# Attention in pairs of heads: GpSimd takes one head at a time, a third buffer for masked scores, and four bursts of half-width matmuls a pair

## What is computed

```
x = x + layernorm(attention(layernorm(x)))
x = x + layernorm(ffn(layernorm(x)))
```

```
q = rmsnorm(h @ Wq_a) @ Wq_b           # 128 features + 64 that are rotated by position (rope)
ckv = h @ Wkv_a;  kv = rmsnorm(ckv[:64]) @ Wkv_b;  k_pe = rope(ckv[64:])   # one k_pe for all heads
scores = (q . k) * 192**-0.5, causal;  p = softmax(scores);  o = p @ v;  out = concat(o) @ Wo
```

## Time and profile before

| | |
|---|---|
| median of 3 runs | 632.92 us (631.91 to 633.07) |
| the profiled execution | 632.73 us, of which its span is 630.8 us |
| mean granted clock of TensorE | 0.984 |
| PE busy | 590.5 us (94%) |
| DVE busy | 461.4 us (73%) |
| ACT busy | 400.0 us (63%) |
| POOL busy | 198.9 us (32%) |

### The profile page before, as it was taken

The page is one execution under the profiler, slowest core; times in us unless marked ns, Lnnn a source line. Parts: engine busy times, 40 slices in busy tenths (PEclk is TensorE's granted clock), DMA queues, the critical chain, the costliest instruction groups (busy, mean ns, idle before and its releaser), DMA issues.

```text
span 630.8 us, 10967 instructions
## 1 busy us (share of the span) xinstructions
PE 590.5 (94%) x3336; PEld 427.7 (68%) x3336; DVE 461.4 (73%) x1235; ACT 400.0 (63%) x1157; POOL 198.9 (32%) x172
## 2 busy tenths in 40 slices
PE   4786999999999999999999999999989999978996
PEld 4675767677677676776776767767658888754564
DVE  5876677677776777777767777777867888878466
ACT  4454677777777677766776777668753545264343
POOL 3134333443344334433353444344000000024630
PEclk9898999999999999999999999999989999999998
DMA  8100212312132122221331213205465000001003
GB/s 316 31 1 16 87 47 89 95 54 71 56 104 78 48 84 76 78 72 52 97 89 48 82 55 101 71 19 153 154 209 226 2 0 2 0 30 50 1 14 121
DMA packets 19561, 46.93 MB, mean 74 GB/s; under 512 B 2608, under 2 KB 3120, under 8 KB 19248
## 3 DMA queue, kind: packets, MB, share of 16 engines
q1 hardware_dynamic: 19504, 46.23, 22.8%
HBM read 39.80 MB, written 6.42 MB: 73 GB/s over the span
## 4 chain that ended last, share of the span: by engine, by line
PE 50%; issue 15%; DVE 15%; POOL 9%; ACT 9%; DMA 1%; POOLq 0%; SPq 0%; DVEq 0%; ACTq 0%
PE bank L1017 11%; PE bank L1019 9%; PE bank L1018 9%; PE bank L1072 7%; PE bank L1060 6%; POOL qrot L325 6%; ACT pr L407 3%; POOL qt_lo L332 3%; PE bank L1087 3%; DVE qswp L664 2%; DVE qrot L669 1%; DVE ss L677 1%; ACT pt L415 1%; DVE dot L865 1%; ACT qt_hi L397 1%
## 5 line engine op out<-in xcount | busy, mean ns | idle before, releaser
L677 DVE CUSTOM_DVE_ANT_0 ss<-bank,cst 128x128 f32<-128x128 f32 (+3 forms) x256 | 124.2, 490 | 95.6 <-PE bank L1019 75.0
L415 ACT ACTIVATE pt<-bank 128x128 f32<-128x128 f32 (+3 forms) x256 | 110.3, 431 | 88.4 <-PE bank L1060 88.3
L325 POOL TENSOR_TENSOR qrot<-qrot,qswp 64x512 f32<-64x512 f32 x64 | 81.9, 1280 | 208.2 <-DVE qrot L669 208.1
L407 ACT ACTIVATE pr<-ss,small 128x128 f32<-128x128 f32 (+3 forms) x256 | 142.4, 556 | 4.2 <-DVE small L677 4.0
L1060 PE MATMUL bank<-ident,pr 128*128 128x128 f32 x640 | 117.1, 281 | 0.6 <-ACT pr L407 0.6
L1017 PE MATMUL bank<-kt_hi,qt_hi 128*128 128x128 f32 (+3 forms) x256 | 101.0, 395 | 7.9 <-DVE small L677 4.5
L1060 PEld LDWEIGHTS bank<-ident,pr 128*128 128x128 f32 x640 | 74.5, 141 | 49.5 <-ACT pr L407 28.8
L332 POOL TENSOR_TENSOR qt_lo<-qrot,qt_hi 128x512 fp32r<-128x512 f32 x64 | 82.0, 1290 | 29.2 <-ACT qt_hi L397 27.9
L1072 PE MATMUL bank<-pt,kvn 128*64 128x256 f32 (+3 forms) x512 | 86.2, 448 | 0.7 <-ACT pt L415 0.7
L1019 PE MATMUL bank<-kt_hi,qt_lo 128*128 128x128 f32 (+3 forms) x256 | 82.9, 324 | 0.0
L1018 PE MATMUL bank<-kt_lo,qt_hi 128*128 128x128 f32 (+3 forms) x256 | 82.7, 323 | 0.0
(11 more groups left out here) (163 smaller groups left out, 1072.5 us busy)
## 6 DMA issues: line engine op xcount, KB each, us to landing
sv<-sv SPq DMA_DIRECT2D x16, 576.0 KB, 5.0
rsb<-rinv_scratch SPq DMA_DIRECT2D x64, 128.0 KB, 2.9
sq<-sq SPq DMA_DIRECT2D x16, 448.0 KB, 3.3
wvo_scratch<-vs SPq DMA_DIRECT2D x16, 256.0 KB, 4.8
wv_raw<-wvo_scratch SPq DMA_DIRECT2D x8, 512.0 KB, 4.8
xa<-x SPq DMA_DIRECT2D x8, 256.0 KB, 5.0
x<-x SPq DMA_DIRECT2D x1, 2048.0 KB, 9.6
out<-yo SPq DMA_DIRECT2D x8, 256.0 KB, 2.0
```

The lines of the kernel that those rows point to most:

```text
L325: nc.gpsimd.tensor_tensor(qrot[RKV:P, h, :], qrot[RKV:P, h, :], qswp[RKV:P, h, :], ALU.add)\
L407: nc.scalar.activation(pr[:, k % 4, 0:n], ss[:, k % 2, 0:n], ACT.Exp, bias=negmax[:, k % 8:k % 8 + 1], scale=-1.0, accum_out=rsum[:, k:k + ...
L415: nc.scalar.activation(pt[:, b, h, 0:i + 1, i * P:(i + 1) * P], bank[2 + k % 2][:, 0:(i + 1) * P].rearrange("p (j q) -> p j q", q=P), ACT. ...
L677: nc.vector.tensor_tensor_reduce(out=ss[:, k % 2, 0:n], in0=bank[k % 2][:, 0:n], in1=mask[:, SEQ - n:SEQ], scale=-SCALE, scalar=3.4e38, op ...
```

## The change

It has four parts. (1) POOL works head by head: add, then subtract, for head 0, then for head 1. (2) ACT makes the high part of head 0 one step earlier (k = 1 and 9 for 2 and 10; not so in the first half of the first pair), and copies `vs` at step 10 for 9. (3) `ss` has three buffers, chosen by `RING`; DVE waits for the exponents only where the buffer was used two units ago (k = 1 and 15). The third buffer takes room that was left free. (4) On PE, the last three blocks of `output` for sequence 1 stand together in step 2 (were: one in step 2, two in step 3), and `absorb_output` stands in step 9 directly ahead of `output` (was: step 8).

```diff
+RING = (0, 1, 2, 0, 1, 2, 0, 1, 2, 0, 1, 2, 0, 1, 2, 1)
+BACK = [next(d for d in range(1, 17) if RING[k - d] == RING[k]) for k in range(16)]
...
-    ss = att.take("ss", [P, 2, SEQ])
+    ss = att.take("ss", [P, 3, SEQ])
...
-    att.at += 32 + 4 * QB * 2 * RKV
+    att.at += 32
...
                 for b in (1,) if last else (1, 0):
-                    gi = 4 * p + (2 if b else 4)
-                    pool.wait_ge(a.qt_split, gi)
                     for h in range(2):
-                        add_rotated(gi + h, h)
-                    for h in range(2):
-                        query_lo(gi + h, b, h, gi + 2)
+                        gi = 4 * p + (2 if b else 4) + h
+                        pool.wait_ge(a.qt_split, gi)
+                        add_rotated(gi, h)
+                        query_lo(gi, b, h, gi + 1)
...
-                nc.scalar.activation(pr[:, k % 4, 0:n], ss[:, k % 2, 0:n], ACT.Exp, bias=negmax[:, k % 8:k % 8 + 1],
+                nc.scalar.activation(pr[:, k % 4, 0:n], ss[:, RING[k], 0:n], ACT.Exp, bias=negmax[:, k % 8:k % 8 + 1],
...
-                    if k in (2, 4):
-                        h = (k - 2) // 2
+                    if k in ((2, 4) if first else (1, 4)):
+                        h = k // 4
                         query_hi(4 * p + 2 + h, 1, h, None if first else PU * (p - 1) + UNITS + QB * (h + 1))
-                    if k in (10, 12) and not last:
-                        h = (k - 10) // 2
+                    if k in (9, 12) and not last:
+                        h = k // 12
                         query_hi(4 * p + 4 + h, 0, h, PU * p + QB * (h + 1))
-                    if k == 9:
+                    if k == 10:
                         act.wait_ge(a.wvo_made, p + 1)
...
-                if not first:
+                if BACK[k] == 2 and not first:
                     dve.wait_ge(a.exp_made, U - 1)
-                nc.vector.tensor_tensor_reduce(out=ss[:, k % 2, 0:n], in0=bank[k % 2][:, 0:n], in1=mask[:, SEQ - n:SEQ],
+                nc.vector.tensor_tensor_reduce(out=ss[:, RING[k], 0:n], in0=bank[k % 2][:, 0:n], in1=mask[:, SEQ - n:SEQ],
...
                     if k == 2 and not first:
-                        output(2 * p - 1, 1, [1])
-                    if k == 3 and not first:
-                        output(2 * p - 1, 1, [2, 3])
-                    if k == 8:
+                        output(2 * p - 1, 1, [1, 2, 3])
+                    if k in (5, 7) and not last:
+                        query(4 * p + 4 + k // 7, 0, k // 7, p + 1)
+                    if k == 9:
                         if last:
                             pe.wait_ge(a.wvo_moved, p)
                         else:
                             pe.wait_ge(a.wq_split, p + 2)
                         absorb_output(p)
-                    if k in (5, 7) and not last:
-                        query(4 * p + 4 + k // 7, 0, k // 7, p + 1)
-                    if k == 9:
                         output(2 * p, 0, [0], first)
```

## The result

| | before | after |
|---|---|---|
| median of 5 runs, us | 632.71 (631.54 to 633.07) | 635.46 (634.38 to 635.77) |
| span of the profiled execution, us | 630.8 | 632.6 |
| mean granted clock | 0.984 | 0.989 |
| a pair from the middle of the attention, us | 25.33 | 25.73 |

The ratio of after to before is 1.0047, with a 95% interval of 1.0034 to 1.0060. The forecast was 636.4 us and 25.7 us a pair.

A forecast was written before the change was run, and what follows sets the result against it. PE's list was taken to set the pace. Pair 0 at -1.6, pairs 1 to 14 at +0.41 each (+5.7) and pair 15 at -0.4 gave +3.7 us on 632.73, so 636.4 us; range 622 to 641.

The forecast's parts named there:

- The collision in `weights_lo`: Pairs 1 to 14: POOL's `query_lo` holds up DVE's subtractions with both inputs in SBUF, 0.95 us a pair.
- place A: PE's wait in step 5: scores of unit 7 held by unit 5's masking; expected to start 0.95 us later.
- The burst of step 2: Step 3's two `output` blocks join step 2's: 0.24 to 0.3 us less, waited off in step 5, counted 0.
- Place B: PE's wait in step 6: scores of unit 8 wait for head 0's `query_lo`; 0.3 us goes in pairs 1 to 14.
- The burst of step 9: `absorb_output` joins `output` in step 9 on PE: 0.24 us less in all 16 pairs.
- The sum of a pair: Pairs 1 to 14: +0.95 - 0.30 - 0.24 = +0.41 us each, +5.7 in all.
- The buffers: Third buffer removes most of DVE's wait for ACT (19.5 us in 31 places); PE waits in neither, counted 0.
- The first pair: Pair 0: PE starts 1.4 us earlier by POOL's order, and `absorb_output` brings 0.24: -1.6 us.
- The last pair: Pair 15, without `weights_lo`: 0.24 us for `absorb_output`, perhaps step 2's burst too; -0.4 us taken.
- rival 1: POOL comes first each time: 1.16 us a pair for 0.95, 639.3 us in all; chance 15%.
- rival 3: PE's longer idle makes the granted clock fall in half of the pairs: +12 us, 648 us; chance 6%.
- Rival 2: DVE's two subtractions get through before POOL starts: -0.54 us a pair, 623.1 us in all; chance 18%.

The follow-up runs named there:

- e1: Changed kernel with DVE's `weights_lo` doing its two subtractions from SBUF ahead of the two from the PSUM bank; 621.94 us, ratio to before 0.985.
- e2: Changed kernel with ACT making the high part of head 0 in step 2 again in the first half; 624.18 us, ratio to before 0.9875.
- e4: Kernel before with the PE bursts alone joined, and the copy of `vs` in step 10 for 9; 631.03 us, ratio to before 0.998.
- e6: e1 with `rotate_own` of head 1 put behind the masking of unit 5, not ahead of it; 615.22 us, ratio to before 0.9728.
- e8: e3 with, in the second half, ACT's high part of head 0 at k = 9 and the `vs` copy at k = 10; 626.71 us, ratio 0.9907.
- e5: e1 with two buffers for masked scores in place of three; 621.67 us, ratio to before 0.9835.
- e7: Changed kernel with ACT's high part of head 0 ahead of `weights_hi` in step 1; 629.10 us, ratio to before 0.9951.
- e3: Kernel before with POOL's order alone changed: add and subtract, head by head; 633.40 us, ratio to before 1.0024.

## Why the prediction was right

Mechanism, place and size of what decides held. By its own steps, of which the seventh and the ninth were wrong:

1. *The collision in `weights_lo`, +0.95 a pair.* Shown, at 0.98 (e1) and 0.99 (e2). The starts were placed on the same 0.01 us, and DVE went first by 0.01 or 0.02 in all 14 pairs: the first of the two subtractions took 0.29, POOL went in between, and the second ended 0.15 behind POOL. That DVE and not POOL was first is luck: the rows gave no reason for it, since the first pair shows only that POOL gets in between. What hung on it was 0.95 or 1.16, not the direction. The Trainium skill (SBUF — State Buffer, section "Who interferes with whom") says that a DVE instruction with two SBUF inputs contends with a GpSimd instruction that reads SBUF, and that the order of issue decides who blocks. The timeline agrees (0.29 for the one that was first, 1.28 for the one behind POOL), and in e1 and e2, where the two don't meet, both take 0.29. The section also says that a DVE instruction with at most one SBUF input does not contend with GpSimd; e1 agrees, where the rests from a bank ran beside POOL at their usual 0.29.
2. *It goes straight into place A.* Shown: the scores of unit 7 come 2.42 behind those of unit 6, for 1.15. That is 1.27, the 0.98 and the 0.29 of the next point.
3. *The burst of step 2, counted 0.* Shown by e4 (place A grows by the 0.29 saved) and e6 (a pair is shorter by all that place A loses).
4. *Place B, -0.30.* Shown by e8 at 0.30 (0.31 by the table), with no new wait behind it.
5. *The burst of step 9, -0.24.* Shown at 0.25: 3.67 for 3.92 from unit 10 to unit 12, in every kernel that has it. In e1 it and place B at 0.33 are the whole of the 0.58 under before.
6. *The sum of a pair, +0.41.* Measured +0.40 to +0.41: +1.27 in place A, -0.29, -0.32 and -0.25 for the rest.
7. *The buffers.* Their effect on the time was rightly 0 (e5), but the sentence that most of DVE's wait goes was wrong. The same wait over the whole span, to be held against the 19.5 in 31 of the earlier trace rows:

```profile
DVE ss L678 <- ACT pr L408: 18.2, 30, 0.6
```

   I read "31 times" as an average over all units. It is two places a pair, and these are k = 15 and k = 1, exactly where `BACK` is still two. Had I laid the count of the waits beside the list of `RING`, I should have seen that it frees the units that never waited.
8. *The first pair, -1.4 and -0.24.* Its timeline, answering to the earlier trace rows:

```profile
55.37 0.40 PE L1020 MATMUL bank<-kt_hi,qt_lo 128*128 128x512 f32 x1
56.28 1.26 POOL L327 TENSOR_TENSOR qrot<-qrot,qswp 64x512 f32<-64x512 f32 x1
57.13 0.57 DVE L653 TENSOR_TENSOR w_lo<-sq,w_hi 128x128 fp32r<-128x128 f32 x1
57.71 0.29 DVE L654 TENSOR_TENSOR w<-sq,w 64x128 fp32r<-64x128 f32 x1
...
58.05 0.50 PE L1018 MATMUL bank<-ql_hi,w_hi 128*128 128x512 f32 x1 [2.29 <-DVE w L654]
```

   POOL's addition for head 1 goes from 56.28 to 57.54. Only L653 is held by it, 0.28 us, as foreseen, and PE's wait is 2.29 instead of 3.75: 1.46 less, for 1.4.
9. *The last pair, -0.4.* Wrong: it takes about 0.14 more. The burst of step 2 does count, since place A has no `weights_lo` there (-0.29). But in step 8 PE now reaches its next transpose before the exponents are there, 0.86 behind L1020, where the first transposes of the earlier trace rows stand 0.17 behind the same kind of matmul. Before, `absorb_output` stood in that gap and covered it. The stretch from unit 7 to the last scores is 0.43 longer than before (12.84 for 12.41) although the burst of step 9 brings -0.24, so the wait costs 0.67. In the middle pairs two `query` blocks of steps 5 and 7 stand ahead of this point, which the last pair lacks. The timeline of step 8 there:

```profile
446.30 0.34 PE L1020 MATMUL bank<-kt_hi,qt_lo 128*128 128x384 f32 x1
447.16 0.27 PE L1082 MATMUL bank<-ident,small 128*8 128x128 f32 x1 [0.53 <-ACT pr L408]
```

   I had asked what covers step 8 for the middle pairs only.

The total, from the scores of unit 7 in the first pair to the last unit of the last: -1.46 and -0.24, 14 times +0.406, and +0.14 are +4.1. The two profiled executions differ by +4.2 over that stretch, for a forecast of +3.7. Their spans differ by less, +1.8, and the medians by +2.75, since three stretches outside it go the other way in these two executions:

- 1.04 up to the first scores (45.05 and 44.01). The code of that stretch is the same in all these kernels. It goes with the granted clock, which was at half for 6.83 us from 26.55 before, and for 3.41 us from 28.20 after; e4, with 6.83 as well, reaches the first scores at 45.27, and e7, with none ahead of them, at 43.02. Why the clock differed is open, and it says nothing of the change.
- 0.33 between the first scores and unit 7 of the first pair (11.12 and 10.79). e4, with the old order on POOL, has 11.13, and e3, with the new one alone, 10.91. So some 0.2 of it is a gain of POOL's order that my sum left out.
- 1.10 behind the attention. The windows of the same stretch, in the kernel before and then after, columns as in the earlier trace rows:

```profile
466.87:470.28 3.41, 3.31 (x8) 2.65 (x9) 2.60 (x5) 2.10 (x3) 0.00 (x0) 0.50 0.81 187
```

```profile
466.87:470.28 3.41, 0.81 (x4) 0.38 (x3) 1.58 (x3) 0.00 (x0) 0.00 (x0) 1.00 0.62 192
```

Before, the granted clock stood at half (1.2 GHz) for these 3.41 us; after, it stayed at full (2.4 GHz). No edit here was made to test this, and it isn't explained. The +2.75 of the medians lies between the +1.8 and the +4.2, so the closeness of 636.4 to 635.46 is in part luck: by the attention alone the kernel after would stand at 636.9.

Of the rivals, rival 1 (POOL first, 25.9 a pair) and rival 3 (the clock: it is 1.00 through all middle pairs, though PE stands 1.53 us in each) did not come. Rival 2's numbers did, in e1 and e2: the case in which the two don't meet, forecast at -0.54 a pair, measures -0.58. In e1 they miss each other by 0.03 us.

## What to carry to other kernels

When work is moved onto GpSimd at an earlier time, lay its start and end against VectorE's instructions with two SBUF inputs, and follow the one that may be held to the next wait of TensorE; if they meet, change VectorE's order so that the ones with a PSUM input fall beside GpSimd, which here turned a loss of 0.5% into a gain of 1.5% with one line. Do this for every place where the two engines' lists run side by side, the first and the last round too: the same line cost 0.6 us in the first pair. A saving on the busiest engine ahead of one of its waits is worth nothing until that wait is shortened, and the edit that shortened it (masking ahead of rotation) brought 0.59 us a pair, as much as all four parts of the change without the collision (0.58). Before a buffer is added, see which units wait, and whether the new ring gives those units a longer distance.

## What the runs showed of the hardware

- GpSimd's instruction that started 0.02 us behind L653 took 1.42 us in the trace, and 1.28 in e1 and e7, where nothing was in its way. An excess of 0.14 on GpSimd's side is all that shows there of a collision that costs VectorE 0.98; reading GpSimd's rows alone, one would pass over it.
- A GpSimd instruction that is waiting gets in between two VectorE instructions that stand 0.31 us apart from start to start and belong to the same engine's queue (313.57, 313.88): GpSimd doesn't wait until VectorE runs out of such work.
- TensorE stood idle 2.60 us at about 470 us in the changed kernel, and the granted clock did not fall:

```profile
470.04 0.50 PE L1018 MATMUL bank<-wv,o_s 128*128 128x512 f32 x1 [2.60 <-DVE wv L704]
```

  In the first pair it stood 2.29 us until 58.05, and there the clock was at half for 3.4 us from 58.92. In the kernel before it stood 2.37 us until 466.97, with the clock at half from 466.87; in e2 1.74 us until 433.47, with the clock at half from 434.90. So the length of the idle time alone doesn't tell whether the clock falls.
